# A two-layer graph network on one core: gather groups begun by leave of SyncE instead of behind a memset

## The chip, the core and the metric

One NeuronCore of a Trainium2 chip. Its engines run apart and meet through semaphores: TensorE (PE, its weight loads PEld), VectorE (DVE), ScalarE (ACT), GpSimd (POOL) and SyncE (SP). POOL issues the gathers (indirect DMAs that fetch one row of a table for each of 128 indices), SP issues the plain DMAs. The metric is the device time of one execution in microseconds, the median of several.

## What is computed

The reference, cut to what matters (12,500 nodes of 64 features, 212,500 edges sorted by `dst`, 16 edge types):

```python
h = jnp.maximum(_layernorm(x, axis=-1), 0.0)
# layer 0: one 64x64 weight per edge type
msg = sum over r of (h[src] * (etypes == r)[:, None]) @ weight[r]
x = x + segment_sum(msg, dst, num_segments=N)
h = jnp.maximum(_layernorm(x, axis=-1), 0.0)
# layer 1: an edge network
msg = relu(concatenate([h[src], h[dst], edge_attr]) @ W1 + b1) @ W2 + b2
x = x + segment_sum(msg, dst, num_segments=N)
```

## The kernel before

The edges are cut into `G` = 208 groups of 1024 (8 tiles of 128), and a turn is `U` = 8 groups, so each layer has `NIT` = 26 turns. For each group POOL issues 8 gathers (`gather`, L710), each of 128 rows of 64 floats, into one of the 8 buffers of `rows`: from `h_table` in the first layer, from `p_table` in the second. The first turns of the first layer are gathered straight by `src_tab`; from group 16 on the indices stand in `idx`, which SP fills four groups at a time (`batch` in the first layer, `load_idx` in the second).

First layer. PE multiplies the gathered rows by one-hot matrices (L1379) into the sums of 256 slots, ACT copies these to `slots` (L890), PE multiplies every second group by the 16 type weights (L1386), ACT copies the result to `nodes_t` (L894), PE places it (L1393) and DVE adds it to the window of `acc`. Once in a turn, behind groups 4 and 7, PE also turns and multiplies a chunk of finished nodes (L1336, L1344), and SP stores the chunk to `p_table` and `q_table` (`store_pq`, L581).

Second layer. For each group PE makes the products of edge attributes and destination terms (L1461, L1462), DVE adds the gathered rows to them (`add_rows`, L1219), ACT takes the relu (L951), PE sums it (L1466), DVE masks and reduces it (L1226, L1230), adds an older window (L1239) and spreads the destination term of the next group but one step on (`spread_q`, L1243), on which PE's next products wait. SP loads the destination windows `q_win` two groups at a time (`load_q`, L642), and for every four groups the indices (L635) and the edge attributes (L626).

What holds POOL back. Before the gathers of group g POOL waits until group g-3 has been consumed (`slots_summed` or `pre_added`), before every fourth group for its indices, and, with `wait_apart(pool, spaced, ...)`, for the end of a memset of its own: behind the eight gathers of a group it clears `spacer`, a tile of 128x512 that nobody reads, and the next group's gathers wait for it. `wait_apart` (L360) is a wait and an increment of a counter that nobody reads; the instructions at L359 beside it work out the value waited for. SP has no part in this: its queue holds only loads and stores, each behind a wait for the consumer that frees the buffer.

## Time and profile before

| | us |
|---|---|
| median of 3 runs (lowest to highest) | 4864.73 (4861.53 to 4864.73) |
| profiled execution, its time | 4855.4 |
| its span | 4853.2 |
| busy: POOL | 3380.0 (70% of the span) |
| busy: PE | 2787.7 (57%) |
| busy: DVE | 1468.1 (30%) |
| busy: ACT | 577.2 (12%) |
| mean granted TensorE clock | 0.692 of full |

The busy shares count compute and gathers; register, branch and semaphore instructions are not counted, and neither is the issue of DMAs on SP. Engine PE's ends are modelled. "Idle before" is the time in which the engine had nothing in work, with what the profile thinks released it; "issue" means that no wait is seen. The first layer's gathers with `idx` run from 215 us to 2443 us, the second layer's from 2470 us to 4837 us.

### The profile page before, as it was taken

What the parts mean: (1) busy time and instruction counts of PE and PEld (TensorE: products, weight loads), DVE (VectorE), ACT (ScalarE), POOL (GpSimd) and SP (SyncE); (2) the same over time, 40 slices, a digit from 0 to 9 for tenths busy, and PEclk for the clock granted to TensorE, in tenths of its full rate; (3) what the DMA queues carried; (4) which work ended last, traced back from release to release, by engine and by line L of the source; (5) the groups of instructions that cost most, each with busy time, mean ns of one, the idle gap of its engine ahead of it and who ended that gap; (6) DMA issues with size and microseconds to landing.
All of it is one profiled execution on the core that took longest, in us unless ns stands there. A gap on an engine that the chain in (4) does not pass through costs nothing.

```text
span 4853.2 us, 37713 instructions
## 1 busy us (share of the span) xinstructions
PE 2787.7 (57%) x10310; PEld 1549.3 (32%) x10310; DVE 1468.1 (30%) x2002; ACT 577.2 (12%) x1139; POOL 3380.0 (70%) x3742
## 2 busy tenths in 40 slices
PE   2565665656556655656565565565555655656555
PEld 1343343434334433434332232222222222222222
DVE  6322222222222222222232333233332332332333
ACT  3111111111111111111110010010000000100000
POOL 7567667666666666676757767777777777777776
PEclk9777776677767777776766666666666666666666
DMA  4111111111111111111111112111111111211111
GB/s 102 20 27 25 25 27 25 25 27 25 25 25 27 25 26 26 25 25 27 25 29 31 29 31 31 29 31 31 29 31 29 32 31 29 32 31 32 29 31 28
DMA packets 391187, 144.15 MB, mean 30 GB/s; under 512 B 321650, under 2 KB 337323, under 8 KB 391163
## 3 DMA queue, kind: packets, MB, share of 16 engines
q0 software_dynamic: 106304, 109.07, 11.8%
q1 hardware_dynamic: 282245, 34.18, 4.9%
q10 hardware_dynamic: 2614, 0.62, 0.1%
q8 instruction: 10, 0.16, 0.0%
q14 instruction: 14, 0.11, 0.0%
HBM read 129.03 MB, written 12.83 MB: 29 GB/s over the span
## 4 chain that ended last, share of the span: by engine, by line
POOL 39%; issue 26%; another core or an unknown queue 17%; PE 12%; DVE 3%; ACT 1%; SPq 1%; DMA 1%; POOLq 0%; DVEq 0%; ACTq 0%
POOL rows L710 36%; PE ps L1379 4%; PE ps L1386 2%; POOL spacer L763 2%; PE ps L1462 1%; PE ps L1461 1%; PE ps L1393 1%; POOL spacer L743 1%; PE ps L1344 1%; PE ps L1346 1%; DVE z_slot L1230 0%; PE ps L1466 0%; DVE q_blk L1243 0%; DVE slots L1219 0%
## 5 line engine op out<-in xcount | busy, mean ns | idle before, releaser
L710 POOL DMA_INDIRECT rows<-p_table,idx x1661 | 1579.6, 951 | 702.0 <-issue 631.3
L710 POOL DMA_INDIRECT rows<-h_table,idx x1533 | 1452.1, 947 | 693.8 <-issue 506.6
L1461 PE MATMUL ps<-w_attr,attr_t 64*128 64x512 f32 x416 | 400.9, 1063 | 1004.8 <-DVE q_blk L1243 694.7
L1379 PE MATMUL ps<-onehot,rows 128*64 128x256 f32 x3328 | 661.8, 512 | 101.2 <-DMA rows<-h_table,idx 50.8
L1386 PE MATMUL ps<-w_types,slots 128*128 128x128 f32 x3328 | 518.2, 307 | 226.5 <-issue 201.6
L1095 DVE TENSOR_TENSOR onehot<-key,ps 128x2048 f32<-128x2048 f32 x209 | 474.6, 2279 | 439.5 <-remote 389.5
L1386 PEld LDWEIGHTS ps<-w_types,slots 128*128 128x128 f32 x3328 | 462.3, 215 | 314.1 <-issue 282.5
L1219 DVE TENSOR_TENSOR slots<-ps,rows 128x512 f32<-128x512 f32 x208 | 143.9, 692 | 1378.1 <-DMA rows<-p_table,idx 831.5
L1379 PEld LDWEIGHTS ps<-onehot,rows 128*64 128x64 f32 x3328 | 333.6, 179 | 349.4 <-issue 287.8
L1461 PEld LDWEIGHTS ps<-w_attr,attr_t 64*128 64x128 f32 x416 | 96.8, 288 | 1041.8 <-issue 1041.4
L1462 PE MATMUL ps<-q_blk,onehot 128*128 128x512 f32 x416 | 422.2, 1118 | 0.0
L890 ACT COPY slots<-ps 128x512 f32<-128x512 f32 x416 | 239.3, 588 | 1057.9 <-remote 766.6
L1466 PE MATMUL ps<-relus,onehot 128*128 128x512 f32 x416 | 339.8, 913 | 0.9 <-DVE z_blk L1226 0.9
L1158 DVE TENSOR_TENSOR acc<-acc,ps 64x128 f32 x208 | 58.2, 280 | 918.1 <-remote 645.7
L951 ACT ACTIVATE relus<-slots 128x512 f32<-128x512 f32 x208 | 131.1, 630 | 1663.2 <-DVE slots L1219 1511.3
L1393 PE MATMUL ps<-place,nodes_t 128*64 128x256 f32 x416 | 158.6, 521 | 277.8 <-ACT nodes_t L894 142.1
L1230 DVE TENSOR_REDUCE z_slot<-z_blk 128x64 f32<-128x512 f32 x208 | 209.1, 1005 | 0.1
L1226 DVE TENSOR_TENSOR z_blk<-ps,blocks 128x512 f32<-128x512 f32 x208 | 142.8, 687 | 193.5 <-remote 136.7
L1462 PEld LDWEIGHTS ps<-q_blk,onehot 128*128 128x128 f32 x416 | 100.8, 301 | 295.6 <-issue 295.6
L1393 PEld LDWEIGHTS ps<-place,nodes_t 128*64 128x64 f32 x416 | 70.4, 184 | 354.2 <-issue 185.7
L1470 PEld LDWEIGHTS ps<-onehot,z_slot 128*65 128x65 f32 x416 | 95.5, 230 | 231.5 <-issue 229.0
L1456 PEld LDWEIGHTS ps<-q_win,onehot 128*128 128x128 f32 x416 | 110.8, 267 | 176.4 <-issue 176.4
(142 smaller groups left out, 1971.8 us busy)
## 6 DMA issues: line engine op xcount, KB each, us to landing
rows<-p_table,idx POOLq DMA_INDIRECT x1661
rows<-h_table,idx POOLq DMA_INDIRECT x1533
attr<-in_edge_attr_dram SPq DMA_DIRECT2D x52, 128.0 KB
q_win<-q_table SPq DMA_DIRECT2D x208, 32.0 KB
p_table<-pq_out SPq DMA_DIRECT2D x25, 120.0 KB
q_table<-pq_out SPq DMA_DIRECT2D x25, 120.0 KB
out_dram<-xs SPq DMA_DIRECT2D x25, 120.0 KB
xs<-in_x_dram SPq DMA_DIRECT2D x6, 480.0 KB, 6.4
```

Source lines behind the costliest of these rows:

```text
L710: pool.indirect_dma_start(rows[:, u, t, :], None, table, bass.IndirectOffsetOnAxis(ap=at, axis=0)).then_inc(s, 16)
L890: act.copy(to, slot_ps[:, u % 2, t, :].rearrange("p t (r w) -> p t r w", w=W0)).then_inc(slots_copied, 1)
L1095: dve.tensor_tensor(onehot[:, b], key0[:, bass.ds(g, 1), :].rearrange("p a (t c) -> p (a t) c", c=1).broadcast_to([P, T, C0]), iota_ps.rea ...
L1219: dve.tensor_tensor(presum[:, u % 2, 0:T * D], pre_ps[:, u % 2, :], rows[:, u].rearrange("p t d -> p (t d)"), ALU.add).then_inc(pre_added, 1)
L1226: dve.tensor_tensor(by_tile(z_blk[:]), by_tile(z_ps), own_tile, ALU.mult).then_inc(z_masked, 1)
L1230: dve.tensor_reduce(z_slot[:, u, 0:D], z_blk[:].rearrange("p (t d) -> p d t", d=D), X, ALU.add).then_inc(z_slotted, 1)
L1379: last = pe.matmul(slot_ps[t % 2 * D:(t % 2 + 1) * D, b, t // 2, :], rows[:, u, t, :], onehot[:, b, t, :], start=True, stop=True)
L1386: last = pe.matmul(nodes_ps, slots[:, b, r, :], w_types[:, r, :], start=(r == 0), stop=(r == R - 1))
L1393: last = pe.matmul(win_ps, nodes_t[:, h * D:(h + 1) * D], place[:, h, :], start=(h == 0), stop=(h == 1))
L1461: pe.matmul(pre_ps[:, u % 2, :], attr_t[half, u // 2, :], w_attr[half].rearrange("k j d -> k (j d)"), start=True, stop=False)
L1462: pe.matmul(pre_ps[:, u % 2, :], oh1_t[:, u, :], q_blk[:, u % 2, :], start=False, stop=True).then_inc(pre_made, 1)
L1466: pe.matmul(z_ps, oh1[:, u, :], relu_rows[:, u % 2, :], start=True, stop=True).then_inc(z_made, 1)
```

## The change

The memsets and `spacer` go. Instead there are two counters, `asked` and `granted`. At the head of each group (but the first of all) POOL waits for `granted`, then adds one to `asked` for the group after, and then makes its other waits and its gathers as before. SP takes part in each group: it waits for `asked`, adds one 16 times (first layer) or 8 times (second) to a counter `paced` that nobody reads, adds one to `granted`, and only then goes on to what stands next in its queue. SP's loads and stores are the same ones, set between these grants: in the first layer `batch(it, 1)` behind the grant of group 1 of the turn, `store_pq` behind that of group 4, `batch(it + 1, 0)` behind that of group 5; in the second layer the loads that wait for the sum of group g-2 stand behind the grant of group g, for every odd g, and `store_out` behind that of group 1.

```diff
+    PACE = (16, 8)
-        spacer = sb("spacer", [P, T * D], fp32)
-        spaced = sem("spaced")
+        asked = sem("asked")
+        granted = sem("granted")
+        paced = [sem(f"paced_{b}") for b in range(2)]
+        def asks(it, u, second):
+            return (NIT - 2 if second else -2) * U + it * U + u + (0 if second else 1)
...
 # SP, first layer
-                with sp.Fori(2, NIT) as it:
-                    for k in range(U // B):
-                        batch(it, k)
-                    store_pq(it - 2, chunk_nodes)
+                def turn_of_loads(it, last=False):
+                    for u in range(U):
+                        wait_apart(sp, asked, asks(it, u, False))
+                        for _ in range(PACE[0]):
+                            sp.sem_inc(paced[u % 2], 1)
+                        sp.sem_inc(granted, 1)
+                        if u == 1:
+                            batch(it, 1)
+                        if u == 4:
+                            store_pq(it - 2, chunk_nodes)
+                        if u == 5 and not last:
+                            batch(it + 1, 0)
+                        if u == 5 and last:
+                            first_batch(0)
+                batch(2, 0)
+                with sp.Fori(2, NIT - 1) as it:
+                    turn_of_loads(it)
+                turn_of_loads(NIT - 1, last=True)
+                first_batch(1)
...
 # SP, second layer
-                pairs(0)
-                with sp.Fori(1, NIT - 2) as it:
-                    pairs(it)
-                    store_out(it - 1, chunk_nodes)
+                def turn_of_pairs(it, ahead=2, first=False, store=True):
+                    for u in range(U):
+                        if not first or u >= 1:
+                            wait_apart(sp, asked, asks(it, u, True))
+                            for _ in range(PACE[1]):
+                                sp.sem_inc(paced[u % 2], 1)
+                            sp.sem_inc(granted, 1)
+                        if u % 2 == 1 and (not first or u >= 3):
+                            before, v = back(it, u, 2)
+                            loads_after(before, v, ahead if u >= 3 else min(ahead + 1, 2))
+                        if u == 1 and store:
+                            store_out(it - 2, chunk_nodes)
+                turn_of_pairs(0, first=True, store=False)
+                turn_of_pairs(1, store=False)
+                with sp.Fori(2, NIT - 2) as it:
+                    turn_of_pairs(it)
...
 # POOL, first layer (turn_of_rows)
-                        wait_apart(pool, spaced, (it - 2) * U + u + 1)
+                        wait_apart(pool, granted, asks(it, u, False))
+                        if not last or u < U - 1:
+                            pool.sem_inc(asked, 1)
...
-                        pool.memset(spacer[:], 0.0).then_inc(spaced, 1)
...
 # POOL, second layer (turn_of_groups)
-                        wait_apart(pool, spaced, (NIT - 2 + it) * U + u + 1)
+                        if not first or u >= 1:
+                            wait_apart(pool, granted, asks(it, u, True))
+                        if not last or u < U - 1:
+                            pool.sem_inc(asked, 1)
...
-                        pool.memset(spacer[:], 0.0).then_inc(spaced, 1)
```

What stands in a row on the engines, as built. POOL in the second layer's loop, two groups, before (a row is a line of the kernel, an operation, what it writes and reads, and the semaphores it waits for; `pre_added` counts DVE's sums, additions to semaphores are not shown):

```order
L710 DMA rows<-p_table,idx 128x64 [waits pre_added]
L710 DMA rows<-p_table,idx 128x64 x7
L763 MEMSET spacer 128x512
L359 REGISTER_ALU
L359 REGISTER_ALU [waits spaced]
L710 DMA rows<-p_table,idx 128x64 [waits pre_added]
L710 DMA rows<-p_table,idx 128x64 x7
L763 MEMSET spacer 128x512
```

and now:

```order
L743 DMA rows<-p_table,idx 128x64 [waits pre_added]
L743 DMA rows<-p_table,idx 128x64 x7
L365 REGISTER_ALU
L365 REGISTER_ALU [waits granted]
L743 DMA rows<-p_table,idx 128x64 [waits pre_added]
L743 DMA rows<-p_table,idx 128x64 x7
```

The wait stands at the same place; what it waits for is no longer an instruction of POOL's own engine.

SP in the first layer's loop, a whole turn, before:

```order
L590 ISA [waits slots_summed]
L590 DMA idx<-src_tab 128x32
L359 ISA
L590 ISA [waits slots_summed]
L590 DMA idx<-src_tab 128x32
L581 ISA [waits pq_copied]
L581 DMA p_table<-pq_out 120x256
L581 DMA q_table<-pq_out 120x256
L595 REGISTER_ALU
L595 COMPARE_AND_BRANCH
```

and now, the head of the turn, groups 0 to 4 (the 16 additions before each grant are not shown):

```order
L365 REGISTER_ALU [waits asked]
L365 ISA [waits asked]
L596 ISA [waits slots_summed]
L596 DMA idx<-src_tab 128x32
L365 REGISTER_ALU
L365 REGISTER_ALU [waits asked] x2
L587 ISA [waits asked,pq_copied]
L587 DMA p_table<-pq_out 120x256
L587 DMA q_table<-pq_out 120x256
```

Each load and store now has grants ahead of it and behind it in the one queue.

SP in the second layer's loop, before, one odd group's loads and the next wait:

```order
L638 ISA [waits pre_added]
L638 TENSOR_LOAD base_row
L642 ISA
L642 DMA q_win<-q_table 128x64
L642 ISA
L642 DMA q_win<-q_table 128x64
L359 REGISTER_ALU
L638 ISA [waits pre_added]
```

and now:

```order
L660 ISA [waits pre_added]
L660 TENSOR_LOAD base_row
L664 ISA
L664 DMA q_win<-q_table 128x64
L664 ISA
L664 DMA q_win<-q_table 128x64
L365 REGISTER_ALU
L365 REGISTER_ALU [waits asked] x2
L660 ISA [waits pre_added]
```

Between two pairs of loads stand two waits for `asked`, and with each of them a chain of 8 and a grant.

## Rows read from the trace of the kernel before

**Rows 1.** Timeline of POOL, first layer: start, length, operation, idle before and releaser.
```profile
2039.61 0.95 POOL L710 DMA_INDIRECT rows<-h_table,idx  x1 [0.31 <-issue]
2040.56 0.54 POOL L743 MEMSET spacer<- 128x512 f32 x1
2042.06 0.95 POOL L710 DMA_INDIRECT rows<-h_table,idx  x1 [0.96 <-POOL spacer L743]
```
**Rows 2.** Timeline of POOL near the start, groups without a memset between them.
```profile
112.91 0.94 POOL L710 DMA_INDIRECT rows<-h_table,src_tab  x1 [0.30 <-issue]
114.16 0.94 POOL L710 DMA_INDIRECT rows<-h_table,src_tab  x1 [0.30 <-issue]
...
122.91 0.94 POOL L710 DMA_INDIRECT rows<-h_table,src_tab  x1 [0.30 <-issue]
124.16 0.94 POOL L710 DMA_INDIRECT rows<-h_table,src_tab  x1 [0.30 <-issue]
```
**Rows 3.** The memsets of the two layers: count, length in ns, first and last start.
```profile
L743 POOL MEMSET spacer<- x192: 539/544/551, 225.0 to 2443.1; 128x512 f32 x192
L763 POOL MEMSET spacer<- x208: 539/544/551, 2479.4 to 4837.2; 128x512 f32 x104
```
**Rows 4.** Waits, whole span: engine, tile, releaser, total us, times, longest.
```profile
DVE slots L1219 <- DMA rows<-p_table,idx: 831.5, 110, 9.3
PE ps L1379 <- DMA rows<-h_table,idx: 50.8, 19, 7.1
```
**Rows 5.** Timeline of PE and of ACT, first layer, behind group 7 of a turn.
```profile
1337.99 1.13 PE L1379 MATMUL ps<-onehot,rows 128*64 128x256 f32 x4 [0.28 <-issue]
1345.48 1.97 PE L1393 MATMUL ps<-place,nodes_t 128*64 128x256 f32 x4 [6.36 <-ACT nodes_t L894]
...
1345.16 0.27 ACT L894 COPY nodes_t<-ps 128x128 f32<-128x128 f32 x1 [11.59 <-remote]
```
**Rows 6.** Timeline of DVE, second layer, two groups that wait for their gather.
```profile
3484.62 0.69 DVE L1219 TENSOR_TENSOR slots<-ps,rows 128x512 f32<-128x512 f32 x1 [7.85 <-DMA rows<-p_table,idx]
3496.01 0.69 DVE L1219 TENSOR_TENSOR slots<-ps,rows 128x512 f32<-128x512 f32 x1 [7.79 <-DMA rows<-p_table,idx]
```
**Rows 7.** Timeline of PE and of DVE, second layer, one group that waits for no gather.
```profile
3815.10 2.04 PE L1461 MATMUL ps<-w_attr,attr_t 64*128 64x512 f32 x2 [4.14 <-DVE q_blk L1243]
3819.36 1.91 PE L1466 MATMUL ps<-relus,onehot 128*128 128x512 f32 x2
...
3814.26 0.69 DVE L1243 TENSOR_TENSOR q_blk<-ps,blocks 128x512 f32<-128x512 f32 x1 [0.29 <-remote]
3821.31 0.69 DVE L1226 TENSOR_TENSOR z_blk<-ps,blocks 128x512 f32<-128x512 f32 x1 [1.44 <-issue]
3823.07 0.67 DVE L1243 TENSOR_TENSOR q_blk<-ps,blocks 128x512 f32<-128x512 f32 x1
```
**Rows 8.** Line L1219 in one stretch of 103 us and one of 253 us, with its waits.
```profile
L1219 DVE TENSOR_TENSOR slots<-ps,rows x11: 691/692/692, 3747.2 to 3849.7; 128x512 f32<-128x512 f32 x11
  DMA rows<-p_table,idx: 13.8, 2
...
L1219 DVE TENSOR_TENSOR slots<-ps,rows x23: 691/692/692, 2605.2 to 2857.9; 128x512 f32<-128x512 f32 x23
  DMA rows<-p_table,idx: 11.7, 2
```
**Rows 9.** Timeline of SP's DMA issues, second layer: start, to the end of the last.
```profile
2493.96 0.85 SPq L642 DMA_DIRECT2D q_win<-q_table  x2
...
3019.32 2.64 SPq L642 DMA_DIRECT2D q_win<-q_table  x2
3022.00 0.77 SPq L635 DMA_DIRECT2D idx<-src_tab  x1
3024.16 0.70 SPq L626 DMA_DIRECT2D attr<-in_edge_attr_dram  x1
3027.01 0.00 SPq L614 DMA_DIRECT2D out_dram<-xs  x1
```

More of the change, by code:

```diff
@@ L594, in _, with first_batch @@
                 sp.dma_start(w_attr[T * F:2 * T * F], w_attr[0:T * F]).then_inc(weights_copied, 16)
[L595 to L600 removed]
+                def first_batch(k):
                     sp.wait_ge(slots_summed, 2 * (AHEAD + G - U + (k + 1) * B))
                     sp.dma_start(idx[:, k * B:(k + 1) * B, :], src_tab[:, k * B:(k + 1) * B, :]).then_inc(batch_in[k], 16)
+                def turn_of_loads(it, last=False):
[17 more added lines that the diff above has]
+                first_batch(1)
                 store_pq(NC - 1, chunk_nodes)
@@ L642, in load_q, with loads_after @@
                         sp.dma_start(q_win[:, v + b, :], q_table[bass.ds(bases[b], P), :]).then_inc(q_in[v + b], 16)
-                def pairs(it, ahead=2):
-                    for u in range(1, U, 2):
-                        g = it * U + u
-                        if ahead or u < V:
-                            wait_apart(sp, pre_added, AHEAD + g + 1)
-                            load_q(g + V - 1, (u + V - 1) % V)
-                        if u % B == B - 1 and (ahead or u < B):
-                            k = u // B
-                            if ahead:
-                                load_idx((it + 1) * U + k * B, k)
-                            if ahead == 1 and k == U // B - 1:
-                                load_last_attr()
-                            else:
-                                load_attr((it + 1) * U + k * B if ahead else 0, k)
+                def loads_after(it, u, ahead=2):
+                    g = it * U + u
+                    if ahead or u < V:
+                        wait_apart(sp, pre_added, AHEAD + g + 1)
+                        load_q(g + V - 1, (u + V - 1) % V)
+                    if u % B == B - 1 and (ahead or u < B):
+                        k = u // B
+                        if ahead:
+                            load_idx((it + 1) * U + k * B, k)
+                        if ahead == 1 and k == U // B - 1:
+                            load_last_attr()
+                        else:
+                            load_attr((it + 1) * U + k * B if ahead else 0, k)
+                def turn_of_pairs(it, ahead=2, first=False, store=True):
[10 more added lines that the diff above has]
+                            store_out(it - 2, chunk_nodes)
                 for k in range(U // B):
@@ L752, in _, with turn_of_groups @@
             with pool.If(fits > 0):
-                def turn_of_groups(it, last=False):
+                def turn_of_groups(it, first=False, last=False):
                     for u in range(U):
-                        wait_apart(pool, spaced, (NIT - 2 + it) * U + u + 1)
+                        if not first or u >= 1:
+                            wait_apart(pool, granted, asks(it, u, True))
+                        if not last or u < U - 1:
+                            pool.sem_inc(asked, 1)
                         if u == 0:
@@ L762, in turn_of_groups @@
                             gather(p_table, u, j, rows_in[u])
-                        pool.memset(spacer[:], 0.0).then_inc(spaced, 1)
-                with pool.Fori(0, NIT - 1) as it:
+                turn_of_groups(0, first=True)
+                with pool.Fori(1, NIT - 1) as it:
                     turn_of_groups(it)
```

7 lines of the change are left out of this document (2 added, 5 removed).

## Prediction

> **What bounds the kernel now.** I read the page's busy shares first: POOL is the busiest engine, but a share over two layers says nothing of who waits for whom. So next the timeline of POOL over the end of one group [rows 1]. The eighth gather runs 0.95 us, the memset follows without a gap, and the next group's first gather starts 1.50 us behind the memset's start (2040.56 to 2042.06). Where no memset stands between groups, gathers start every 1.25 us straight across the group's border, though the first gather of a group carries a wait there too: from 112.91 to 122.91 eight gathers take 10.00 us, and the idle time ahead of the ninth is the same 0.30 us as ahead of the others [rows 2]. So POOL needs 10.0 us for a group's gathers, and 1.50 - 0.30 = 1.2 us more with the memset and the wait for it: 11.2 us. What the kernel takes for a group comes from the first and last memset of each layer [rows 3]: (2443.1 - 225.0) / 191 = 11.61 us in the first layer, (4837.2 - 2479.4) / 207 = 11.39 us in the second. POOL with its border accounts for 11.2 of both, so POOL sets the pace, and 0.4 and 0.2 us are something else.
>
> The question is how far behind POOL the next engine stands, so the third view is who waits for the gathers [rows 4]. In the first layer PE waits for them only 50.8 us in all, 19 times: PE and what hangs on it need almost the whole 11.6 us themselves. In the second layer DVE waits for them 831.5 us in 110 of 208 groups. There POOL bounds, at least in every second group.
>
> **The change, part by part.**
>
> The memset and the wait for it go. 398 borders (191 + 207) at 1.2 us are 478 us. This is the ceiling, reached only if nobody else needs more than 10.0 us for a group.
>
> What POOL gets instead is a wait for `granted`, an addition to `asked` and the same other waits. Rows 2 show that a satisfied wait at the border costs nothing, since POOL's queue has handed out the last gathers before they run. I take 0; if POOL's queue should be empty then, the price is what stands between the end of the memset and the next gather today, 0.96 us [rows 1], which leaves a gain of only 0.2 us a group. I take 0 because the leave for a group is asked for a whole group earlier.
>
> What SP gets: a wait, 16 or 8 additions and a grant for each group. No row of before shows a bare addition on SP, so I bound it by SP's bursts [rows 9]. Two loads of `q_win` with what stands between them (four instructions with the register moves) take 0.85 us in a quick burst, 0.21 us each; in a slow one the same takes 2.64 us, and from its first load at 3019.32 to its last DMA at 3027.01 there are some 12 instructions in 7.69 us, 0.64 us each. A chain of 16 is then 3.4 to 10.3 us, a chain of 8 1.7 to 5.1 us. Leave is asked one group ahead, so a grant has about 10 us to come: at 0.21 us it is never late, at 0.64 us it is close. Lengths between the ends I take as hidden in both layers, nearer the quick end for the chain alone, since a chain moves no data.
>
> The Trainium skill (Advanced Engine Details and Errata, Miscellaneous Facts, Network/Comms) gives 50 to 100 ns for reading a semaphore from a sequencer. An estimate from that page would make the chain of 16 0.8 to 1.6 us and the grants free; no row here shows such an instruction alone, and the slow burst in rows 9 speaks for far more.
>
> SP's old work moves: in the first layer POOL may start group 2 of a turn only when SP has seen group 7 of the turn before summed, issued its load and run a chain. POOL waits for that same sum anyway, so this costs the load and the chain, 4 to 11 us, on a group that has two groups of about 10 us gathered ahead of it. I take 0. In the second layer the loads of group g-2 stand between the grants of g and g+1; the heaviest burst (7.7 us) and two chains of 8 (10.3 us) are 18.0 us, against 20 us for two groups at POOL's own pace. I take 0 here too, and keep the other end for a rival.
>
> **First layer, what is late next.** With POOL at 10.0 us PE no longer waits for gathers: at most 50.8 us. I take half, 25 us. The reason is a turn's worst place [rows 5]: PE's records end at 1339.1 and it then idles 6.36 us for `nodes_t`, but ACT's copy itself started only at 1345.16, released by nothing in the rows. So part of what looks like idle PE is PE's work that is not over.
>
> The Trainium skill (Perfetto Trace Analysis, Per-engine timelines) says the same: a matmul's end in the profile is estimated from its size, not observed. By this page the gain of the first layer would be nearer 0 than 50.8; by the waits alone it would be 50.8.
>
> **Second layer, what is late next.** The loop that then decides runs from one `q_blk` of DVE to the next [rows 7]: 0.84 us to PE's products (3814.26 to 3815.10), 4.26 to the sum over the relus (3819.36), 1.95 to DVE's mask (3821.31), 1.76 through window and reduction to the next `q_blk` (3823.07), together 8.8 us. In groups that wait for their gather, one add follows the other after 11.4 us, with 7.8 us of DVE's waiting in it [rows 6]. But 8.8 us is a simple group; others turn one-hots, attributes or a chunk of output. Two stretches in which the gathers were seldom late show the rest [rows 8]: 10 steps in 102.5 us with 13.8 us of waiting for gathers, (102.5 - 13.8) / 10 = 8.9 us; and 22 steps in 252.7 us with 11.7 us of it, 241.0 / 22 = 10.95 us. Nothing in the rows says why the second is slow. POOL cannot go below 10.0, so over the two stretches I expect (10 x 10.0 + 22 x 10.95) / 32 = 10.65 us for a group. That is 11.39 - 10.65 = 0.74 us less, by 207: 153 us.
>
> **The sum.** 25 + 153 = 178 us off the profiled execution's 4855.4 us, 4677 us. The median of the runs stands 9 us higher (4864.7), so 4687; I say 4690. The two ends without trouble on SP: nothing gained, 4865; and second layer at 10.0 us (1.39 x 207 = 288) with the whole 51 of the first, 339, 4526.
>
> **The rivals.**
>
> *The gathers still bound.* The second layer runs at POOL's 10.0 to 10.2 us throughout. For it: 831.5 us of waiting, and a loop of 8.8 us. Against it: the slow stretch of rows 8. Time 4530 to 4590. Chance 0.12.
>
> *The rest of the loop needs all of the time.* PE, DVE and ACT run in the second layer as in the slow stretch, at 11 us or more, as soon as nobody makes them wait. For it: that stretch, and the first layer, which is nearly so already. Against it: the stretch at 8.9. With 11.39 and nothing in the first layer 4865; within 0.2%. Chance 0.13.
>
> *SP sets the pace, and the kernel is slower.* Mechanism: each group of the first layer needs about 20 instructions of SP in one row (the wait with its register work, 16 additions, the grant). At 0.64 us they take 12.8 us, over the 11.61 of today; POOL then stands still for `granted`, and 1.2 x 191 = 229 us are added. It decides from 11.61 / 20 = 0.58 us an instruction. In the second layer two groups need about 24 such instructions (15.4 us) and the loads, 5.5 us in the middle and 7.7 at most: 10.4 to 11.6 us a group, from the 153 us gained to 33 lost. Together 4865 + 229 - 153 = 4940 up to 4865 + 229 + 33 = 5125. For it: rows 9, where slow bursts are what the second layer shows nearly everywhere. Against it: those bursts are full of DMA issues, a chain is not, and a POOL that stands still may relieve what slows SP. Chance 0.29.
>
> That the leave holds nothing back, since a grant is always there before POOL asks its queue for it, is part of my forecast: then the change is simply the memset's removal.
>
> **How the numbers follow.** My forecast (4600 to 4800) has 0.46. The range for 8 in 10 leaves out the lowest part of the first rival and the upper half of the third: 4560 to 4950. A measurement of this kernel can tell about 0.2%, 10 us, from no change. Faster by more: 0.46 + 0.12 = 0.58; within: 0.13; slower: 0.29.
>
> **What would show it.** Right: at the borders in the second layer the gather's idle time reads 0.30 us, POOL's gathers of eight starts stand 10.0 us apart in stretches, DVE's waiting for gathers falls well under 831.5 us while PE's waiting for `q_blk` stays; in the first layer PE's 50.8 us go to nearly nothing and the layer's length hardly moves. Wrong by SP: POOL idles several us at borders with no consumer late, every group, most in the first layer, and groups there last over 12 us. Wrong by the loop: POOL idles at borders with a consumer late, and adds stand 11 us apart without waiting for gathers. Wrong to the good side: DVE waits for gathers in most groups still, 10 us apart.

## The result and the profile after

| | us |
|---|---|
| kernel before, median of 4 runs (lowest to highest) | 4864.4 (4861.5 to 4864.7) |
| changed kernel, median of 4 runs | 5121.6 (5101.7 to 5124.9) |
| ratio, 95% interval | 1.0522 (1.0494 to 1.0549) |
| profiled execution of the changed kernel, time and span | 5101.7, 5099.6 |

Slower by 5.2%, where 4690 us and a range of 4560 to 4950 us had been given. That is the time on the chip of this comparison, the *first chip* from here on; its number is not recorded. The experiments ran on eight other visits to chips. On two of them the changed kernel itself ran, 11.3% faster than the kernel before, and on five more the kernels closest to it were faster by the same; the eighth was like the first. Both halves have to be explained, and only one of them is in the trace of the changed kernel.

That trace first. Where POOL's gathers lie, one line for each layer (duration in ns min/median/max, first and last start in us), in the changed kernel:

```profile
L743 POOL DMA_INDIRECT rows<-p_table,idx x1661: 939/945/1520, 2589.9 to 5072.9; - x185
L743 POOL DMA_INDIRECT rows<-h_table,idx x1533: 939/945/1102, 215.5 to 2559.9; - x192
```

The 192 groups of the first layer take 2344.4 us, 12.2 each, and the 208 of the second 2483.0 us, 11.9 each. Both layers are over the 11.61 and 11.39 us of [rows 3], by much the same: neither the stand-still of the first layer nor the gain of the second that were forecast came.

The borders between groups are as forecast, and the groups are not. Timeline of POOL over such a border and over the next but one:

```profile
3495.75 0.95 POOL L743 DMA_INDIRECT rows<-p_table,idx  x1 [0.30 <-issue]
3497.01 0.95 POOL L743 DMA_INDIRECT rows<-p_table,idx  x1 [0.30 <-issue]
...
3515.77 0.94 POOL L743 DMA_INDIRECT rows<-p_table,idx  x1 [0.30 <-issue]
3524.23 0.94 POOL L743 DMA_INDIRECT rows<-p_table,idx  x1 [7.51 <-SPq L687]
```

At 3497.01 a group begins 0.30 us behind the gather before it, and the 1.2 us of [rows 1] are gone. At 3524.23 POOL has stood still for 7.51 us, released by SP's grant (L687). In the second layer it is so throughout: three groups take 10.0 to 10.8 us each and the next one 15 to 16, twice in a turn (medians by the group's place in the turn). Waits of the changed kernel, whole span (total us, times, longest):

```profile
DVE slots L1256 <- remote: 439.4, 42, 19.7
...
POOL rows L743 <- SPq L687: 340.5, 56, 17.0
...
DVE slots L1256 <- DMA rows<-p_table,idx: 277.7, 44, 9.8
...
PE ps L1416 <- DMA rows<-h_table,idx: 145.4, 29, 7.5
```

L1256 is the addition that was L1219, and L1416 the sum that was L1379. DVE waits for gathers 277.7 us where it was 831.5, and PE waits for them more than before, 145.4 us where it was 50.8 [rows 4]. These totals are what the profile can put down to gathers; much of the record of their landings is missing here, as told below. And DVE waits 439.4 us for something that the profile calls "remote", up to 19.7 us at a time; in the kernel before it was 275.2 us, at most 10.2 at a time.

What SP does meanwhile, by the additions of the second layer's chains (L686) in two stretches, 3488.5 to 3497.5 us and 3523.35 to 3523.85 us:

```profile
L686 SPq EVENT_SEMAPHORE  x8: 5/700/726, 3488.9 to 3496.6; - x8
```
```profile
L686 SPq EVENT_SEMAPHORE  x8: 17/17/17, 3523.4 to 3523.8; - x8
```

The same eight additions take 7.7 us while POOL gathers, and 0.4 us while POOL stands still. Over the whole trace (399 chains) one addition follows the other after 0.07 us where POOL has been still for 2 us, and after 0.6 to 1.0 us on the mean where it has been gathering for more than 12 us.

And the "remote" wait, in the same stretch. Timeline of PE, ACT and DVE: the product that the addition waits for, a copy that waits for an earlier transposition of PE, the addition itself, and then the same product and addition once more, right after POOL's pause:

```profile
3495.25 2.07 PE L1499 MATMUL ps<-q_blk,onehot 128*128 128x512 f32 x2
...
3502.97 0.59 ACT L984 COPY onehot<-ps 128x512 f32<-128x512 f32 x1 [13.27 <-issue]
...
3512.77 0.69 DVE L1256 TENSOR_TENSOR slots<-ps,rows 128x512 f32<-128x512 f32 x1 [19.04 <-remote]
...
3526.60 2.07 PE L1499 MATMUL ps<-q_blk,onehot 128*128 128x512 f32 x2
...
3528.71 0.69 DVE L1256 TENSOR_TENSOR slots<-ps,rows 128x512 f32<-128x512 f32 x1 [4.23 <-PE ps L1499]
```

By its records PE has the first product at 3497.32, and the addition starts at 3512.77, 15.4 us later; the second product is there at 3528.67, and the addition starts 0.04 us later. I call this the *lateness* of a PE result. The trace also holds PE's own increment of the semaphore for the first product: it is at 3512.74, 15.4 us behind the end of the record and 0.02 us ahead of DVE's addition. So DVE did not notice late; PE's signal came late. With no end of a record near the increment, the profile calls the wait "remote".

Here is the mean lateness, taken for every operation of DVE and ACT that waited at least 0.3 us and for PE, sorted by how many gathers had started in the 20 us before it (16 is gathering without a pause):

| gathers in 20 us | 8, 9 | 10, 11 | 12, 13 | 14, 15 | 16, 17 |
|---|---|---|---|---|---|
| changed kernel, first chip: mean lateness, us | 0.3 | 0.7 | 1.8 | 4.8 | 8.5 |
| kernel before, first chip | | | 2.0 | 3.5 | |
| changed kernel, chip 3 | | | | 0.04 | 0.65 |

The figures of single cells hang on how the waits are counted: other ways of doing it give 0.2 to 0.8, 0.9 to 2.2, 2.4 to 3.2, 3.6 to 4.4 and 6.8 to 10.1 us for the first row. The rise from left to right stays in all of them. The 0.65 us of chip 3 are mostly gathers that ended last; of the waits for PE alone the mean is 0.08 us there and the longest 0.18. Averaged over all such waits, the lateness on the first chip hardly differs between the kernels (3.0 us before, 3.3 changed). What grows are the long ones: over 10 us late are 27 results of 868 in the kernel before and 111 of 901 in the changed one.

It is PE's results alone. Where ACT waits for DVE, in the same traces, it starts 0.04 to 0.05 us behind DVE's end on the mean, on the first chip as on chip 3.

So on the first chip two things go with unbroken gathers: SP's instructions are some ten times as long, and PE's results come up to 20 us late. The trace alone can't say which of them costs the time, nor whether the gathers are their cause.

### The profile page after: what moved, and what is told of

It is laid out like the page before. It is cut to its first block, busy times and chain, and to the rows that moved or that the text cites. A ratio compares the mean times of both kernels' runs of the same rounds, so it can differ in the third digit from the quotient of the medians.

```text
span 5099.6 us, 43549 instructions
## 1 busy us (share of the span) xinstructions
PE 2721.3 (53%) x10310; PEld 1547.8 (30%) x10310; DVE 1471.1 (29%) x2002; ACT 577.1 (11%) x1139; POOL 3158.2 (62%) x3342
## 3 DMA queue, kind: packets, MB, share of 16 engines
q0 software_dynamic: 106304, 109.07, 11.3%
## 4 chain that ended last, share of the span: by engine, by line
issue 32%; another core or an unknown queue 24%; PE 19%; SPq 9%; POOL 7%; DVE 6%; DMA 2%; DVEq 1%; ACT 0%; POOLq 0%; ACTq 0%
POOL rows L743 7%; PE ps L1416 5%; PE ps L1423 4%; SPq L609 4%; PE ps L1499 3%; PE ps L1498 3%; PE ps L1503 2%; DVE q_blk L1280 1%; DMA rows<-h_table,idx 1%; DVE slots L1256 1%; DVE z_slot L1267 1%; SPq L664 1%; DVEq L1271 1%; SPq L686 1%
## 5 line engine op out<-in xcount | busy, mean ns | idle before, releaser
L1498 PE MATMUL ps<-w_attr,attr_t 64*128 64x512 f32 x416 | 360.6, 962 | 1138.9 <-DVE q_blk L1280 855.3
L1416 PE MATMUL ps<-onehot,rows 128*64 128x256 f32 x3328 | 692.4, 508 | 335.6 <-issue 182.3
L1423 PEld LDWEIGHTS ps<-w_types,slots 128*128 128x128 f32 x3328 | 486.5, 229 | 476.2 <-issue 399.8
L1416 PEld LDWEIGHTS ps<-onehot,rows 128*64 128x64 f32 x3328 | 342.2, 178 | 605.9 <-issue 519.6
L1256 DVE TENSOR_TENSOR slots<-ps,rows 128x512 f32<-128x512 f32 x208 | 143.8, 691 | 1225.7 <-remote 439.4
L1498 PEld LDWEIGHTS ps<-w_attr,attr_t 64*128 64x128 f32 x416 | 85.5, 255 | 1177.2 <-issue 1176.3
L1499 PE MATMUL ps<-q_blk,onehot 128*128 128x512 f32 x416 | 404.9, 1074 | 0.0
L1280 DVE TENSOR_TENSOR q_blk<-ps,blocks 128x512 f32<-128x512 f32 x208 | 141.3, 679 | 119.7 <-remote 98.5
```

Of the source, the lines that this page charges most:

```text
L1256: dve.tensor_tensor(presum[:, u % 2, 0:T * D], pre_ps[:, u % 2, :], rows[:, u].rearrange("p t d -> p (t d)"), ALU.add).then_inc(pre_added, 1)
L1280: dve.tensor_tensor(by_tile(q_blk[:, u % 2, :]), q_ps.rearrange("p (a d) -> p a d", a=1).broadcast_to([P, T, D]), own_tile, ALU.mult).then ...
L1416: last = pe.matmul(slot_ps[t % 2 * D:(t % 2 + 1) * D, b, t // 2, :], rows[:, u, t, :], onehot[:, b, t, :], start=True, stop=True)
L1423: last = pe.matmul(nodes_ps, slots[:, b, r, :], w_types[:, r, :], start=(r == 0), stop=(r == R - 1))
L1498: pe.matmul(pre_ps[:, u % 2, :], attr_t[half, u // 2, :], w_attr[half].rearrange("k j d -> k (j d)"), start=True, stop=False)
L1499: pe.matmul(pre_ps[:, u % 2, :], oh1_t[:, u, :], q_blk[:, u % 2, :], start=False, stop=True).then_inc(pre_made, 1)
```

## The experiments

All times are medians in us, each beside the kernel before on the same chip.

| kernel | chip | time | before | ratio (95% interval) |
|---|---|---|---|---|
| free | 12 | 4208.1 | 4744.3 | 0.8870 (0.8855 to 0.8885) |
| no_chain | 12 | 4208.6 | 4744.3 | 0.8871 (0.8856 to 0.8886) |
| chain2x | 12 | 4208.0 | 4744.3 | 0.8869 (0.8855 to 0.8884) |
| narrow | 12 | 4606.9 | 4744.3 | 0.9709 (0.9693 to 0.9726) |
| after_again | 3 | 4216.1 | 4754.3 | 0.8867 (0.8852 to 0.8881) |
| before_again | 3 | 4757.1 | 4754.3 | one run |
| wide | 3 | 4934.0 | 4754.3 | 1.0377 (1.0360 to 1.0395) |
| chain8x | 3 | 4219.1 | 4754.3 | 0.8874 (0.8859 to 0.8889) |
| chain12x | 13 | 4739.3 | 4754.5 | 0.9969 (0.9959 to 0.9980) |
| free_b | 13 | 4215.0 | 4754.5 | 0.8866 (0.8849 to 0.8884) |
| after_c | 1 | 4215.4 | 4754.4 | 0.8866 (0.8840 to 0.8892) |
| slow_sp | 14 | 4787.7 | 4752.9 | 1.0081 (1.0049 to 1.0113) |
| free_c | 14 | 4214.2 | 4752.9 | 0.8873 (0.8845 to 0.8902) |
| free_d | 5 | 4208.0 | 4744.2 | 0.8870 (0.8844 to 0.8896) |
| late_before | 0 | 4746.2 | 4744.5 | 1.0004 (0.9992 to 1.0015) |
| late_after | 0 | 4215.7 | 4744.5 | 0.8883 (0.8857 to 0.8909) |
| late_slow_sp | 0 | 4923.9 | 4744.5 | 1.0376 (1.0345 to 1.0406) |
| free_e | 7 | 5202.5 | 4855.3 | 1.0713 (1.0672 to 1.0753) |

### No pause and no leave (free), other chains (no_chain, chain2x), a shorter memset (narrow)

free is the kernel before without what the change removes, and without what it puts in its place:

```diff
-                        wait_apart(pool, spaced, (it - 2) * U + u + 1)
...
-                        pool.memset(spacer[:], 0.0).then_inc(spaced, 1)
...
-                        wait_apart(pool, spaced, (NIT - 2 + it) * U + u + 1)
```

no_chain and chain2x are the changed kernel with another `PACE`:

```diff
-    PACE = (16, 8)
+    PACE = (0, 0)      # no_chain; (32, 16) in chain2x
```

narrow is the kernel before with a smaller `spacer`:

```diff
-        spacer = sb("spacer", [P, T * D], fp32)
+        spacer = sb("spacer", [P, D], fp32)
```

> The kernel before without the memset and without the wait for it: POOL waits only for indices and for consumed buffers. Theory A (SP's chains and loads hold POOL back, nothing else is wrong with the change): without them the second layer comes down as forecast, 4600 to 4690 us. Theory B (uninterrupted gathers slow the others: in the trace of the changed kernel a result of PE reaches DVE or ACT 8.5 us late on the mean where 16 or 17 gathers began in the last 20 us, and 0.3 us late where 8 or 9 did; a semaphore instruction on SP takes 0.7 to 1.0 us there against 0.06): taking the pause away from every group gives back what it gains, 4850 to 5100 us, with late results more frequent than in the kernel before.

> The changed kernel with chains of no length: leave, grants and the order of SP's loads stay. Theory A: SP's work before a grant falls from 4.2 us to well under 1 us in the first layer and from 16 us to 8 us in the second, most of the 640 us of POOL's late starts go, and the time falls below that of before, 4600 to 4800 us. Theory B: POOL runs in longer unbroken stretches, results are late more often, and the time stays at 4950 to 5150 us.

> The changed kernel with chains of 32 and 16. Theory A: each late grant comes another 8 to 16 instructions later, at the 0.35 us that a link takes on the mean now: 5.6 us in the first layer at the two late groups of each turn (48 x 5.6 = 270 us) and 2.8 us at 75 of the second (210 us): 5300 to 5600 us. Theory B: a longer chain is also a longer pause of the gathers, in which a link takes only 0.06 us; the time hardly moves or falls, 5000 to 5150 us.

> The kernel before with a memset of 128x64 in place of 128x512: its 0.54 us fall to about 0.1, so the pause between the groups' gathers goes from 1.5 to about 1.05 us, and a group's gathers from 11.2 to 10.75 us. Theory A: the second layer follows POOL, 0.45 x 207 = 93 us off at most: 4770 to 4820 us. Theory B: 4840 to 4950 us, since the shorter pause lets more results be late.

Measured: 4208.1, 4208.6, 4208.0 and 4606.9 us. Neither theory had this. The first three are the same time whatever SP does, 11.3% under the kernel before and far under both theories' figures; and the kernel before itself took 4744 us here, 120 less than on the first chip. So the first thing that differed was the chip. narrow: 137 us less over 399 borders is 0.34 us each, where 0.45 was expected; its memset takes 0.17 us, not the 0.1 that I had assumed.

### The same two kernels on another chip (after_again, before_again), longer chains (chain8x), a longer memset (wide)

after_again and before_again are the two kernels unaltered; chain8x has `PACE = (128, 64)`; wide has

```diff
-        spacer = sb("spacer", [P, T * D], fp32)
+        spacer = sb("spacer", [P, 2 * T * D], fp32)
```

> The changed kernel itself, unaltered, once more. With doubled chains and with none it took 4208 us on a chip on which the kernel before took 4744 us. Theory C (the chip, or what ran beside it, decides: where a link of SP's chain takes 0.06 us at any time, SP is never late): 4200 to 4215 us where the kernel before takes about 4744 us, and about 5100 us again where it takes about 4860 us. Theory D (chains of 16 and 8 alone fall badly in time): over 5000 us on any chip.

> The kernel before, unaltered, for a trace from the same chip as the other runs. Theory C: POOL's groups stand 11.2 us apart in both layers with nothing lost to late consumers (11.61 and 11.39 in the first trace), the results of PE are seldom over 1 us late, and SP's bursts are quick throughout. Theory D: the trace looks like that of the first chip.

> The kernel before with a memset of 128x1024 instead of 128x512: 0.53 us more on each of 399 borders. Theory C: POOL sets the pace alone, 4744 + 212 = 4956 us where the kernel before takes 4744; where it takes 4860, a longer pause relieves the others and less than 212 us is added. A pause that protects the other engines: no more time at all, or less.

> The changed kernel with chains of 128 and 64. At 0.06 us a link they take 7.7 and 3.8 us of the 10.0 us that a grant has: Theory C on an undisturbed chip: still never late in the second layer, and late by little in the first, where a turn has two stops for consumers: 4208 to 4350 us. On a chip with links of 0.35 us and more (45 us a chain) over 7000 us.

Theory C holds: 4216.1 us for the changed kernel (4200 to 4215 expected), 0.887 of the kernel before, and chains eight times as long cost 3 us. wide costs 180 us, 0.45 us a border (0.53 expected): with nobody else late, every pause is simply paid. The lines of the changed kernel's gathers on this chip, in the same view as above:

```profile
L743 POOL DMA_INDIRECT rows<-p_table,idx x1661: 943/947/1277, 2122.1 to 4198.4; - x185
L743 POOL DMA_INDIRECT rows<-h_table,idx x1533: 943/947/1199, 176.1 to 2093.0; - x192
```

9.98 us a group in both layers: POOL never waits. Its waits in the same trace, with the longest wait for a grant 0.3 us:

```profile
DVE slots L1256 <- DMA rows<-p_table,idx: 1340.0, 206, 7.2
...
POOL rows L743 <- issue: 1006.5, 3301, 0.3
...
PE ps L1416 <- DMA rows<-h_table,idx: 701.3, 183, 7.4
...
POOL rows L743 <- SPq L610: 3.0, 10, 0.3
```

PE and DVE wait for gathers in nearly every group even at 10.0 us; in the kernel before on the first chip it was PE 19 times and DVE 110 [rows 4]. SP's additions take 0.06 us, gathers or not (the stretch from 2200 to 2300 us):

```profile
L686 SPq EVENT_SEMAPHORE  x80: 17/17/17, 2207.2 to 2291.4; - x80
```

The kernel before on the same chip (the same view of its gathers):

```profile
L710 POOL DMA_INDIRECT rows<-p_table,idx x1661: 943/947/1258, 2375.7 to 4738.1; - x185
L710 POOL DMA_INDIRECT rows<-h_table,idx x1533: 943/947/1192, 175.8 to 2347.9; - x192
```

11.31 and 11.36 us a group, close to 11.2 but for 0.8 to 1.1 us more at one group of each turn and 0.1 to 0.3 at two others, which go too when the memset does. That the first layer took 11.6 on the first chip was the chip's doing. The second layer of the kernel before is as long there (2366.5 us from first to last gather) as here (2362.4): with the pause in place, PE's late results cost that layer next to nothing.

One mark of the first chip stands on the page, in the section on DMA issues (last column: median us from issue to landing). The kernel before there, then on chip 3:

```profile
rows<-p_table,idx POOLq DMA_INDIRECT x1661
```
```profile
rows<-p_table,idx POOLq DMA_INDIRECT x1661, 2.4
```

On the first chip the landing of the gathers could not be told. Its traces hold 13327 semaphore updates by DMAs (kernel before) and 12219 (changed kernel), the others some 60000 for the same work. The engines' own updates are fewer as well: 4431 in the kernel before, 7494 on chip 3.

### Chains as long as the first chip's (chain12x), and the search for a second such chip (free_b, after_c)

chain12x has `PACE = (192, 96)`; free_b is free, after_c the changed kernel.

> The changed kernel with chains of 192 and 96, which puts the slow links of the first chip's SP (0.7 us) on an undisturbed chip (0.062 us a link) by number: 192 x 0.062 = 11.9 us a chain in the first layer, 5.9 us in the second. Theory E (chains alone can make the kernel slower, as the rival put it, once one takes longer than POOL's 10.0 us): the first layer is paced by them at 12.2 us a group, 192 x 2.2 = 420 us more, the second layer stays at 10.0: 4640 us where the changed kernel takes 4216. Theory F (the first chip's slowdown came through SP's chains alone): with links as slow as there the whole of 5120 us comes back. On a disturbed chip: over 8000 us.

> The kernel before without memset and without its wait, once more, on whichever chip it meets. On an undisturbed chip 4208 to 4220 us again. On one like the first (kernel before at 4860 us, links of SP at 0.7 us while gathers run, PE's results up to 20 us late): if SP's grants are what costs there, 4530 to 4690 us; if unbroken gathers slow PE's results as well, 4850 to 5100 us with no grant anywhere.

> The changed kernel, unaltered, on one more chip. Three chips so far gave the kernel before 4744 to 4755 us, and one of them the changed kernel 4216; the first gave 4864 and 5122. If the first chip was the odd one: 4205 to 4220 us beside about 4750 again. If the chip is one like the first: 5100 to 5125 beside about 4860, with links of 0.7 us while gathers run.

chain12x: 4739.3 us, where theory E had 4640. The first layer now runs from 173.9 to 2612.9 us, 12.7 us a group (12.2 expected; the excess stands behind the last group of a turn, at 15.3 us), the second at 9.98. So a chain can set the pace, from the point at which it outlasts POOL's 10.0 us. On the first chip most chains did not: a chain of 16 took 5.6 us on the mean, but 26 of the 192 took over 10 us, up to 19.6. And in the second layer chains of 6.0 us lose nothing, where the first chip's were 2.6 us on the mean (29 of 207 over 6, up to 11.2). So steady chains at or over the first chip's mean don't make its second layer, and theory F falls in this form; what single long chains cost there is not shown by it. free_b and after_c met undisturbed chips.

### All of SP as slow as on the first chip (slow_sp), and free again (free_c, free_d)

In slow_sp `PACE` is (192, 96), and the loads of the second layer are put off too:

```diff
                         wait_apart(sp, pre_added, AHEAD + g + 1)
+                        for _ in range(52):
+                            sp.sem_inc(slowed, 1)
                         load_q(g + V - 1, (u + V - 1) % V)
...
+                        for _ in range(38):
+                            sp.sem_inc(slowed, 1)
                         if ahead:
                             load_idx((it + 1) * U + k * B, k)
```

> The changed kernel with chains of 192 and 96 and, in the second layer, 52 more additions ahead of every pair of window loads and 38 more ahead of every load of indices and attributes: on an undisturbed chip (0.062 us an addition) all of SP's work in the loops then takes about as long as it did on the first chip. Theory F (a slow SP alone explains the first chip's changed kernel): first layer 12.75 us a group as with chains of 192 alone, second layer (2 x 6.2 + 3.2 + 2.5 + half of 2.4) / 2 = 9.7 up to 12 us a group, because a pair of groups waits for two chains, the sum and the loads in one row: 5000 to 5150 us. Theory G (there the late results of PE are needed as well): the second layer stays at 10.0 to 10.5 us a group, 4740 to 4850 us.

> The kernel before without memset and without its wait on one more chip. Undisturbed (kernel before at about 4750 us): 4205 to 4220 us. Like the first (kernel before at about 4860 us): 4530 to 4690 us if only SP's grants cost time there, 4850 to 5100 us if unbroken gathers make PE's results late.

> The same kernel (before without memset and wait) on a further chip, in search of one like the first. Undisturbed: 4205 to 4220 us beside about 4750. Like the first: 4850 to 5100 us beside about 4860 if unbroken gathers make PE's results late, 4530 to 4690 if only the grants cost time there.

4787.7 us, theory G: the second layer takes 10.24 us a group (2640.6 to 4770.2), where it took 11.9 on the first chip. A slow SP, alone, gives 1.008 and not 1.052. That is no small cost: it is 572 us over the 4216 of the changed kernel, most of it in the first layer (2438.7 us from first to last gather with `idx`, against 1916.9). But there the chains are twice as long, at 11.8 us, as the 5.6 us that they took on the mean on the first chip, and they are steady where those took from 0.9 to 19.6. It is a harsher SP on the mean, and no copy. free_c and free_d met undisturbed chips once more.

### Late results of PE, put in by hand (late_before, late_after, late_slow_sp)

In all three PE makes one product of the second layer nine times, once in a turn; everything else is the kernel before, the changed kernel, and slow_sp:

```diff
-                    pe.matmul(pre_ps[:, u % 2, :], attr_t[half, u // 2, :], w_attr[half].rearrange("k j d -> k (j d)"), start=True, stop=False)
+                    for n in range(9 if u == 2 else 1):
+                        pe.matmul(pre_ps[:, u % 2, :], attr_t[half, u // 2, :], w_attr[half].rearrange("k j d -> k (j d)"), start=True, stop=u == 2 and n < 8)
```

> The kernel before, with PE's product of edge attributes made nine times instead of once in group 2 of every turn of the second layer (the same values each time): eight more at 1.0 to 2.0 us make PE's result there 8 to 16 us late, once in 91 us. Theory H (late results alone are swallowed by the buffers, three groups deep, as long as PE catches up): 4750 to 4790 us. Otherwise one turn grows by what PE loses, up to 26 x 16 us: 4950 to 5170 us.

> The changed kernel with the same late result. With quick links the grants follow the sum within 1 to 2 us. Theory H: POOL now has 80 us for a turn and PE needs 71 + 8 to 16, so 0 to 7 us a turn are lost: 4216 to 4400 us. If the grants behind late sums cost more than that by themselves: over 4400 us.

> The same late result, in the changed kernel whose chains (192 and 96) and loads are as long in time as on the first chip; without late results it took 4788 us. Theory H (late results and a slow SP together cost more than each alone, because the sum, the loads and the chain stand in one row ahead of a grant): more than the 4788 us plus what late_after adds to 4216, by 5 us or more a turn (130 us): 4950 to 5150 us. If the two only add up: 4788 to 4970 us.

Timeline of DVE in late_after, the additions of a group in time, of the late one and of two behind it:

```profile
3661.37 0.69 DVE L1256 TENSOR_TENSOR slots<-ps,rows 128x512 f32<-128x512 f32 x1 [6.44 <-DMA rows<-p_table,idx]
3682.26 0.69 DVE L1256 TENSOR_TENSOR slots<-ps,rows 128x512 f32<-128x512 f32 x1 [17.29 <-PE ps L1500]
3690.34 0.69 DVE L1256 TENSOR_TENSOR slots<-ps,rows 128x512 f32<-128x512 f32 x1 [3.19 <-PE ps L1500]
3698.24 0.69 DVE L1256 TENSOR_TENSOR slots<-ps,rows 128x512 f32<-128x512 f32 x1 [4.23 <-PE ps L1500]
```

The late addition comes 21 us after the one before it, with 17.29 us of waiting for PE, some 11 us later than in time; and then they follow each other after 8 us until the gathers have been caught up. It costs 2 us in the kernel before (4746.2; 4750 to 4790 expected) and 7 in the changed one (4215.7 beside the 4208 of chips with the same time of before). Behind a slow SP it costs 136: 4923.9 against 4787.7, the second layer at 10.9 us a group instead of 10.24. The time is under theory H's range (4950 to 5150), and inside the one given for a mere adding up; but late_after put the price of the late results at 7 us, so adding up comes to 4795, and 129 us are left over, the 5 us a turn that H had asked for. By that H holds, if narrowly: the sum, the loads and the chain stand in one row ahead of a grant, and a late sum moves them all. Late results once a turn in one layer and a slow SP give 1.038 here. This is no copy of the first chip, whose first layer lost less (12.2 us a group, not 12.7) and whose second layer lost more; it shows that the two together cost more than their sum.

### Unbroken gathers on a chip like the first (free_e)

> The kernel before without memset and wait, a last time, in search of a chip like the first. Undisturbed: 4205 to 4220 us beside about 4750. Like the first: 4850 to 5100 us beside about 4860 if unbroken gathers make PE's results late, 4530 to 4690 if only the grants cost time there.

Chip 7 was one: kernel before at 4855.3 us, no landing times on the page, 12356 semaphore updates by DMAs in the trace. free has no grant, no chain and no new row on SP, and it takes 5202.5 us there, 7.1% over the kernel before; on four other chips the same code is 11.3% under it. The direction is that of late results of PE, whose range (4850 to 5100) it exceeds. Its gathers, and what POOL waits for (whole span):

```profile
L708 POOL DMA_INDIRECT rows<-p_table,idx x1661: 938/944/1483, 2588.4 to 5162.0; - x185
L708 POOL DMA_INDIRECT rows<-h_table,idx x1533: 938/944/1171, 214.9 to 2555.1; - x192
```
```profile
POOL rows L708 <- DVE slots L1212: 510.5, 76, 11.3
...
POOL rows L708 <- PE ps L1372: 275.1, 44, 21.2
```

12.2 and 12.4 us a group: POOL is now held by the consumers themselves. On chip 12 the same two waits of free come to next to nothing:

```profile
POOL rows L708 <- PE ps L1372: 12.8, 42, 0.3
...
POOL rows L708 <- DVE slots L1212: 0.3, 1, 0.3
```

And the mean lateness of PE's results on chip 7 is 0.3 us with 8 or 9 gathers in 20 us, 2.1 with 12 or 13, 5.4 with 14 or 15 and 8.6 with 16 or 17: the rise of the changed kernel's row on the first chip, without any of the change's waits. Over 10 us late are 114 results of 1101. On chip 12 the mean is 0.6 with 16 or 17. SP is slow here too, with no chain at all: two loads of `q_win`, which take 0.85 us on chips 3 and 12 at the median, take 3.5 (2.1 in the kernel before on the first chip). PE's clock does not tell the chips apart: in the second layer the kernel before was granted 0.66 of full on the first chip and 0.65 on chip 3. The changed kernel was granted 0.64 there and 0.67 on chip 3, but by its records PE is busy only 77 us longer, where the time differs by 900.

So the removal of the pause alone makes the kernel slower on such a chip. That it does so through PE's late results is the reading of the traces; no run takes the lateness away there. The leave seems to have given a part of that back, as far as two chips of the kind can be compared: 1.0522 with it, 1.0713 without, intervals apart. Where SP grants late, POOL stands still, and in that time PE's results come at once. How much the late grants cost by themselves there isn't shown: neither no_chain nor the changed kernel met such a chip again.

## Why the prediction was wrong, point by point

**The step that failed.** The forecast read from the trace of before how much time PE, DVE and ACT need for a group, and held it fixed: 11.6 us but for a gain of 25 us in the first layer, 10.65 us in the second. No term stood for consumers that become slower when POOL pauses less. On the first chip they did. From first to last gather with `idx` the first layer went from 2226.9 to 2344.4 us and the second from 2366.5 to 2483.0, 117 us more in each, where 25 and 153 us less had been given. A grant is not needed for it: free_e has 12.2 and 12.4 us a group with nothing but the pause gone.

**The ceiling was too low.** 398 borders at 1.2 us were 478 us. On chip 3 the spans differ by 4754.9 - 4215.4 = 539.5 us; what stood over 11.2 us a group there went as well, some 60 us.

**The leave is free: right on the undisturbed chips, wrong on the first.** POOL waited for grants for 5 us in all on chip 3. On the first the profile puts 349 us down to them; and of POOL's 218 stands of over 1 us, 126 (652 us) ended within 1.5 us of a grant, so the zero may be off by nearly twice that. A late grant can itself stand behind a late sum.

**The price of an addition.** The ends were 0.21 and 0.64 us, from [rows 9], and I took the quick end "since a chain moves no data". Measured: 0.06 us on undisturbed chips, under both ends, and 0.6 to 1.0 us on the first chip while gathers run, about the slow end and over it. The Trainium skill (Advanced Engine Details and Errata, Miscellaneous Facts, Network/Comms) has 50 to 100 ns for reading a semaphore, and by the estimate worked out from it a chain of 16 was to take 0.8 to 1.6 us; chip 3 agrees with 0.9 us, the first chip does not with 5.6. That a chain moves no data had nothing to do with it. Rows 9 showed the same instructions three times as long at one place as at another, which was a property of the chip: on chip 3 that pair of loads takes 0.85 us at nearly all places.

**First layer, 25 us.** On an undisturbed chip the layer gave 2172.1 - 1916.9 = 255 us; on the first it took 117 more. What was misread is [rows 4] and [rows 5], as PE having no time to spare. The same wait in the kernel before on chip 3:

```profile
PE ps L1379 <- DMA rows<-h_table,idx: 870.5, 191, 9.3
```

There the same matmuls leave PE waiting for gathers in nearly every group. ACT's copy 6 us behind PE's last record was a late result of the kind that chip 3 does not have, and the lateness goes with how POOL gathers. The Trainium skill (Perfetto Trace Analysis, Per-engine timelines) does say that a record's end is estimated, not observed; but by the same estimate the matmuls end on time on chip 3.

**Second layer, 10.65 us a group.** Made of a good stretch at 8.9 and a slow one at 10.95, of which I said that nothing in the rows tells why [rows 8]. Lateness was in both, 2.7 us on the mean in the slow one and 2.0 in the good one; on chip 3 DVE waits for nearly every gather and neither stretch exists. The mean came out as 9.98 undisturbed and 11.9 on the first chip: a mean over the stretches took the slow one as fixed, when how slow the consumers are depends on how POOL gathers.

**The rivals.** The third had the sign and, by number, the time (4940 to 5125). Its mechanism isn't needed for it: it asked for an SP that outlasts a group in every group, the chains outlasted 10 us in 26 groups of 192, and the kernel is slower still with no chain and no grant at all, on chip 7. That the number fits is in good part luck. What it had right is the row sum, loads, chain, grant, which costs where sums are late (late_slow_sp). The first rival, gathers still bounding at 10.0 us, is what the undisturbed chips show, at 4216 us and not 4530, because the first layer follows too. The rival that was missing: *the memset is no waste but a pause, in which the others catch up*. For it spoke that the lateness was in the trace of before, 3.0 us on the mean there and 0.1 on chip 3 where only PE was waited for. Its price could have been bounded only upwards from nothing, since nobody gathered without a pause in that trace.

**What would show it.** The marks named for "wrong by SP" (POOL idle at borders, groups over 12 us) were met in part: POOL did stand at borders and the first layer's groups took 12.2 us, but not in every group, and consumers were late too. They could not tell a POOL held by grants from one held by late consumers; a run without grants could.

**Open.** What disturbs the first chip and chip 7, which may be one and the same, is not known. The data packets of the gathers take as long there (median 126 ns for one of 2 KB on the first chip and on chip 3). SP's instructions, which compute nothing, and PE's results are both held back while gathers run, and fewer semaphore updates are on record. It is not simply the path of all semaphores: DVE's results reach ACT as soon there as elsewhere, and what comes late is PE's own increment, while its consumer starts 0.05 us behind it. Whether PE's work or only its signal is held up is open. So is whether the recording itself does it: every time given here comes from an execution whose span the profiler recorded, and the disturbed ones are those with records missing. Whether a longer pause would be faster on such a chip was not tried there: wide met an undisturbed one. No version beats both kernels on both kinds of chip: free and the changed kernel are equal on the undisturbed ones, and the kernel before is the fastest of the three on the other kind.

## What to carry to other kernels

A comparison on one chip is one of chips as much as of kernels: the same change was 1.052 on the first and 0.887 on two others (and free 0.887 on four and 1.071 on one), each interval within 0.4% of its value. Repeat it on several before the sign is believed, and look in the profile for results that are used long after their modelled end, for semaphore instructions of 0.7 us, and for missing landing times. Ask of a pause, before it is taken out as waste, who may catch up in it; and keep what a grant stands behind off the row that begins with a late sum.

## What the hardware showed that I had not expected

- On two of nine visits PE's results were some 8.5 us late on the mean where gathers ran without a pause (up to 20 us), by PE's own increment, while DVE's results were not late. On the first of them, the only one whose kernel had chains, additions on SP took 0.6 to 1.0 us instead of 0.06; on the second SP's loads were four times as long. On the first chip both were gone within a few us of POOL's standing still.
- On undisturbed chips SP adds to a semaphore every 0.06 us, so that chains of 128 in a group of 10 us cost 3 us in 4216.
- A single result 11 us late in each turn costs nothing (1.0004) where buffers are three groups deep and the consumers can catch up at 8 us a group.
